# Last layer of a graph network: dot products over halves of a turn, additions interleaved, chain operations joined, eight tail buffers

## The reference, cut to what matters

```
def _agg(entity_emb, relation_emb, head, tail, relation_type):
    head_emb, tail_emb, rel_emb = entity_emb[head], entity_emb[tail], relation_emb[relation_type]
    ricci = _l2_normalize(tail_emb + rel_emb)
    hyper_head = expmap0(head_emb)
    hyper_tail = expmap(tail_emb, hyper_head)
    hyper_rel = expmap(rel_emb, hyper_head)
    res = project(mobius_add(hyper_tail, hyper_rel))
    res = logmap(res, hyper_head) + ricci * 1e-07
    res = jax.nn.relu(res)
    sums = jnp.zeros((n_entities, res.shape[-1]), res.dtype).at[head].add(res)
    ...
```

## Time and profile before

| what | value |
|---|---|
| timed, median of 3 runs | 5223.61 us (5222.07 to 5224.58) |
| profiled execution, span | 6351.7 us |
| DVE busy | 3726.5 us, 59% |
| POOL busy | 3463.1 us, 55% |
| PE busy | 2842.1 us, 45% |
| ACT busy | 1728.7 us, 27% |

### The profile page before, as it was taken

How to read it: one execution, slowest core, us unless ns; L and a number is a source line. 1 busy time by engine, 2 the same in 40 slices (tenths; PEclk the granted TensorE clock), 3 DMA queues, 4 the chain that set the end, 5 groups by cost and what they waited for, 6 DMA issues and landing times. The chain is left out here.

```text
span 6351.7 us, 75027 instructions
## 1 busy us (share of the span) xinstructions
PE 2842.1 (45%) x17919; PEld 2271.2 (36%) x17920; DVE 3726.5 (59%) x6870; ACT 1728.7 (27%) x5084; POOL 3463.1 (55%) x3375
## 2 busy tenths in 40 slices
PE   4544588433343334477614434434431343444442
PEld 1333456223333333345403333333331233333332
DVE  6444544255555666444426776667673767667678
ACT  0255200011111111000003354344340335445434
POOL 5667445466555663544265565566525556556551
PEclk7655699666666666678855555555555555555555
DMA  3720400355555554400021111111102111111110
GB/s 101 171 94 1 127 1 1 105 154 172 167 171 169 173 173 143 139 4 1 8 49 42 37 42 37 37 41 38 33 10 50 40 37 42 37 39 41 41 30 13
DMA packets 470914, 446.71 MB, mean 70 GB/s; under 512 B 113322, under 2 KB 417773, under 8 KB 470268
## 3 DMA queue, kind: packets, MB, share of 16 engines
q1 hardware_dynamic: 230602, 227.94, 12.4%
q0 software_dynamic: 116768, 136.51, 9.0%
q10 hardware_dynamic: 123282, 79.08, 4.5%
HBM read 306.93 MB, written 136.34 MB: 70 GB/s over the span
## 5 line engine op out<-in xcount | busy, mean ns | idle before, releaser
L2412 POOL DMA_INDIRECT tg<-tab_d,tail_ids x1632 | 1711.2, 1049 | 1191.1 <-DVEq L2731 644.9
L458 POOL DMA_INDIRECT sorted_edges_d<-place_batch x784 | 825.0, 1052 | 657.1 <-issue 220.6
L2437 PE MATMUL hr<-near_table,near_hot 128*128 x4896 | 654.4, 278 | 926.2 <-issue 593.1
L1598 POOL DMA_INDIRECT xg<-tab_d,src_i x784 | 768.0, 980 | 501.1 <-issue 241.6
L2445 PE MATMUL acc<-msg,sum_hot 128*96 128x65 f32 x3264 | 559.8, 364 | 902.1 <-ACT msg L2519 701.3
L2437 PEld LDWEIGHTS hr<-near_table,near_hot 128*128 128x128 f16 x4896 | 505.6, 108 | 1075.7 <-issue 970.2
L2445 PEld LDWEIGHTS acc<-msg,sum_hot 128*96 128x96 f32 x3264 | 536.4, 277 | 924.8 <-issue 924.7
L2492 ACT ACTIVATE pr<-hr 128x396 f32<-128x396 f32 x576 | 272.2, 482 | 1235.0 <-DMA b2col<-in_L_gnn_be_dram 786.9
L2513 ACT ACTIVATE pr<-pr,coef_c 128x64 f32<-128x64 f32 x1496 | 380.7, 340 | 82.4 <-issue 79.4
L2506 ACT ACTIVATE msg<-tg,coef_b 128x64 f32<-128x64 f32 x1632 | 399.1, 340 | 2.6 <-DVEq L2926 2.6
L2743 DVE TENSOR_REDUCE scal<-prod 128x17 f32<-128x1088 f32 x288 | 370.5, 1286 | 9.8
(11 more groups left out here) (504 smaller groups left out, 5392.9 us busy)
## 6 DMA issues: line engine op xcount, KB each, us to landing
ex<-spread_d SPq DMA_DIRECT2D x112, 448.0 KB
msg_d<-back ACTq DMA_DIRECT2D x112, 448.0 KB
near_hot<-head_row_d SPq DMA_DIRECT2D x96, 408.0 KB
tg<-tab_d,tail_ids POOLq DMA_INDIRECT x1632
spread_d<-zeros ACTq DMA_DIRECT2D x28, 896.0 KB
spread_d<-zeros SPq DMA_DIRECT2D x28, 896.0 KB
idsU<-dst_short_d SPq DMA_DIRECT2D x112, 224.0 KB
pairs_d<-pair_m SPq DMA_DIRECT2D x3, 4800.0 KB
```

The source lines that it names most:

```text
L458: l.eng.indirect_dma_start(K.sorted_edges[:, :], bass.IndirectOffsetOnAxis(ap=K.batch[:, n % 2, 0, k:k + 1], axis=0), K.batch[:, n % 2, 1, ...
L1598: l.eng.indirect_dma_start(xg[j.c % ROWS][:, half * H + k, :], None, K.tab1, bass.IndirectOffsetOnAxis(ap=src_i[:, t:t + 1], axis=0)).then ...
L2412: e.indirect_dma_start(tg[:, u % TAILS * GQ + k, :], None, K.tab3, bass.IndirectOffsetOnAxis(ap=K.tail_ids[:, u * GQ + k:u * GQ + k + 1], ...
L2437: ins = e.matmul(hr[(u * FILLS + g) % 2][:, c:c + PW3], near_hot[u % HOTS][:, k, :], rows[:, bass.ds(at[k] + n * PW3, PW3)], start=n == 0, ...
```

## The change

1. `TAILS` is 8 in place of 9. Four quarters are then always contiguous in `tg`, and a turn's tails are one slice `T_`.
2. `dot` goes over halves: one product of 128x2176 and one reduction for two quarters. `prod` is one tile of the size of the former two. The marks stay as many: one after each half.
3. `gather_up` handles a whole turn. The quarter's operations are split (`sum_keys`, `add_heads`, `add_kinds`), and between the two additions of a quarter stands another operation: the `sum_hot` of the next quarter, a `near_hot`, or its own `sum_hot`.
4. In the chain, operations of the same kind on neighbouring rows of `scal` are joined, some rows are moved so that they are neighbours, and the copies into `scal` are three in place of ten; one of them copies the heads' squared lengths (`PP`), which were read with a stride of 132 elements before. B and C are written to one tile, `coef_bc`.

```
-TAILS = 9
+TAILS = 8
...
+        def gather_up(p, n, mark):
+            sum_keys(p)
+            add_heads(p)
+            sum_keys(p + 1)
+            add_kinds(p)
+            mark()
+            add_heads(p + 1)
+            if n is not None:
+                near(n)
+            add_kinds(p + 1)
+            mark()
+            if n is not None:
+                near(n + 1)
+            for u in (p + 2, p + 3):
+                add_heads(u)
+                sum_keys(u)
+                add_kinds(u)
+                mark()
...
-            def dot(n, x, y, quarters, taken=False, landed=False):
-                for q in quarters:
-                    u = now + q
+            def dot(n, x, y, halves, taken=False, landed=False):
+                for h in halves:
+                    at = slice(2 * h * GQ, (2 * h + 2) * GQ)
+                    u = now + 2 * h + 1
                     if taken:
                         v.wait_ge(near_taken, (u + 1) * FILLS)
                     if landed:
-                        v.wait_ge(got[u % TAILS], 16 * GQ * (u // TAILS + 1))
+                        for w in (u - 1, u):
+                            v.wait_ge(got[w % TAILS], 16 * GQ * (w // TAILS + 1))
                     v.wait_ge(l.sem, l.done())
-                    tt_(prod[q % 2][:, :, :], x(q), y(q), MUL)
+                    tt_(prod[:, :, :], x[:, at, 0:D], y[:, at, 0:D], MUL)
                     v.wait_ge(l.sem, l.done())
-                    v.tensor_reduce(sc[:, n, q * GQ:(q + 1) * GQ], prod[q % 2][:, :, :], AX.X, ADD).then_inc(l.sem, l.add(1))
-                    if q % 2 == 1:
-                        mark()
+                    v.tensor_reduce(sc[:, n, at], prod[:, :, :], AX.X, ADD).then_inc(l.sem, l.add(1))
+                    mark()
...
-            tt0(a2, a2, u2, MUL)
-            tt_(b2, b2, u2, MUL)
+            ab2 = sc[:, 10:14, :].rearrange("p (n two) m -> p n two m", two=2)
+            tt_(ab2, ab2, u2.unsqueeze(1).to_broadcast([P, 2, 2, M]), MUL)
...
-            for c in (cA, cB, cC):
-                tt_(c, c, f, MUL)
+            tt0(abc, abc, three(f), MUL)
```

More of the change, by code:

```diff
@@ L2343, in edge_loop3 @@
     tg = sb("tg3", [P, TAILS * GQ, RW], F32)
-    prod = two("prod3", [P, GQ, D], F32)
+    prod = sb("prod3", [P, 2 * GQ, D], F32)
     msg = [sb(f"msg3{q}", [P, GQ, D + 1], F32) for q in range(QN)]
@@ L2347, in edge_loop3 @@
     cA, cB, cC = (sc[:, n, :] for n in (26, 27, 28))
-    kB, kC = (two(n, [P, M], F32) for n in ("coef_b", "coef_c"))
-    terms = prod[0][:, :, :].rearrange("p k f -> p (k f)")[:, 0:9 * M].rearrange("p (n m) -> p n m", m=M)
+    coef_bc = two("coef_bc", [P, 2, M], F32)
+    kB, kC = ([c[:, n, :] for c in coef_bc] for n in range(2))
+    terms = prod[:, :, :].rearrange("p k f -> p (k f)")[:, 0:9 * M].rearrange("p (n m) -> p n m", m=M)
     zero = pr[1][:, 0:2, :].rearrange("p k f -> p (k f)")[:, 0:256].bitcast(F16)
@@ L2569, in near, with sum_keys @@
             v.tensor_scalar(hot, hot, K.lane_id[:, 0:1], None, ALU.is_equal).then_inc(near_made, 1)
-        def gather_up(u):
-            s, t = turn(u)
+        def sum_keys(u):
             if u >= 2:
@@ L2576, in gather_up, with add_heads @@
                             names.unsqueeze(1).to_broadcast([P, GQ, BN]), ALU.is_equal).then_inc(sum_made, 1)
-            p_, r_, out = pr[s][:, t, 0:D], pr[s][:, t, RW:RW + D], msg[u % QN][:, :, 0:D]
+        def add_heads(u):
+            s, t = turn(u)
+            p_, out = pr[s][:, t, 0:D], msg[u % QN][:, :, 0:D]
             tt_(p_, p_, kA[s][:, t].unsqueeze(2).to_broadcast([P, GQ, D]), MUL)
@@ L2581, in gather_up, with add_kinds @@
             tt_(out, out, p_, ADD)
+        def add_kinds(u):
+            s, t = turn(u)
+            r_, out = pr[s][:, t, RW:RW + D], msg[u % QN][:, :, 0:D]
             if u < QUARTERS - QN:
@@ L2698, in vector, with form @@
         both = lambda x: x.unsqueeze(1).to_broadcast([P, 2, M])
-        def form(out, A, B, C, PP_, pt, pr, tr, q2):
+        def form(out, abc, heads, tr, q2):
+            A, B, C = (abc[:, n, :] for n in range(3))
             x = [terms[:, n, :] for n in range(9)]
-            tt0(x[0], B, pt, MUL)
-            tt0(x[1], C, pr, MUL)
-            tt0(x[2], A, PP_, MUL)
+            tt0(terms[:, 0:3, :], abc, heads, MUL)
             tt0(x[3], C, tr, MUL)
-            tt0(x[4], B, q2[:, 0, :], MUL)
-            tt_(x[5], C, C, MUL)
+            tt_(terms[:, 4:6, :], abc[:, 1:3, :], q2, MUL)
             l.eng.wait_ge(l.sem, l.done())
-            tt0(x[6], x[0], x[1], ADD)
+            tt0(x[6], x[1], x[2], ADD)
             st0(x[7], x[3], 2.0, x[4], MUL, ADD)
-            tt_(x[8], x[5], q2[:, 1, :], MUL)
+            tt_(x[8], x[5], C, MUL)
             l.eng.wait_ge(l.sem, l.done())
-            st0(x[0], x[6], 2.0, x[2], MUL, ADD)
+            st0(x[0], x[6], 2.0, x[0], MUL, ADD)
             tt_(x[1], B, x[7], MUL)
@@ L2738, in dot @@
                     if landed:
-                        v.wait_ge(got[u % TAILS], 16 * GQ * (u // TAILS + 1))
+                        for w in (u - 1, u):
+                            v.wait_ge(got[w % TAILS], 16 * GQ * (w // TAILS + 1))
                     v.wait_ge(l.sem, l.done())
-                    tt_(prod[q % 2][:, :, :], x(q), y(q), MUL)
+                    tt_(prod[:, :, :], x[:, at, 0:D], y[:, at, 0:D], MUL)
                     v.wait_ge(l.sem, l.done())
-                    v.tensor_reduce(sc[:, n, q * GQ:(q + 1) * GQ], prod[q % 2][:, :, :], AX.X, ADD).then_inc(l.sem, l.add(1))
-                    if q % 2 == 1:
-                        mark()
+                    v.tensor_reduce(sc[:, n, at], prod[:, :, :], AX.X, ADD).then_inc(l.sem, l.add(1))
+                    mark()
                 v.wait_ge(l.sem, l.done())
-            head = lambda q: P_[:, q * GQ:(q + 1) * GQ, 0:D]
-            kind = lambda q: R_[:, q * GQ:(q + 1) * GQ, 0:D]
-            tail = lambda q: tg[:, tails(now + q), 0:D]
+            T_ = tg[:, s * M:(s + 1) * M, :]
             def ask_scalar(k):
@@ L2756, in ask_scalar @@
                 v.wait_ge(answered, j * NA + k)
[L2757 to L2768, removed]
+            dot(dPR, P_, R_, range(2), taken=True)
+            dot(dPT, P_, T_, range(1), landed=True)
+            dot(dTR, T_, R_, range(1))
+            if not first:
+                gather_up(p, None if last else n, mark)
+            else:
+                near(n)
+                near(n + 1)
+                v.sem_inc(paced, QN)
+            dot(dPT, P_, T_, range(1, 2), landed=True)
+            dot(dTR, T_, R_, range(1, 2))
             PT, PR, TR, d2 = A1(dPT), A1(dPR), A1(dTR), A2(dPT)
-            q2, n2, s2, t2, u2, a2, b2, X2 = A2(24), A2(2), A2(4), A2(6), A2(8), A2(10), A2(12), A2(14)
+            PP, heads, abc = A1(dPT - 1), sc[:, dPT - 1:dPT + 2, :], sc[:, 26:29, :]
+            q2, n2, s2, t2, u2, a2, b2, X2 = A2(2), A2(24), A2(4), A2(6), A2(8), A2(10), A2(12), A2(14)
             ask = A2(0)
             om = A1(23)
[L2773 to L2778, removed]
+            both_of = lambda x: x.rearrange("p k c -> p c k")
+            v.tensor_copy(sc[:, 2:25:22, :], both_of(T_[:, :, D:D + 2]))
+            v.tensor_copy(sc[:, 3:26:22, :], both_of(R_[:, :, D:D + 2]))
+            v.tensor_copy(PP, PP_)
             ts_(om, PP_, -1.0, 1.0, MUL, ADD)
@@ L2793, in vector @@
             tt0(a2, t2, u2, ADD)
-            tt_(X2, u2, both(PP_), MUL)
+            tt_(X2, u2, both(PP), MUL)
             l.eng.wait_ge(l.sem, l.done())
@@ L2803, in vector @@
             mark()
-            tt0(a2, a2, u2, MUL)
-            tt_(b2, b2, u2, MUL)
+            ab2 = sc[:, 10:14, :].rearrange("p (n two) m -> p n two m", two=2)
+            tt_(ab2, ab2, u2.unsqueeze(1).to_broadcast([P, 2, 2, M]), MUL)
             l.eng.wait_ge(l.sem, l.done())
             tt0(t2, b2, d2, MUL)
-            tt_(u2, a2, both(PP_), MUL)
+            tt_(u2, a2, both(PP), MUL)
             l.eng.wait_ge(l.sem, l.done())
@@ L2841, in vector @@
             mark()
-            tt0(A1(6), A1(6), A1(18), MUL)
-            tt_(A1(7), A1(7), A1(18), MUL)
+            tt_(A2(6), A2(6), both(A1(18)), MUL)
             l.eng.wait_ge(l.sem, l.done())
[L2845 to L2848, removed]
+            tt_(sc[:, 25:29, :].rearrange("p (n two) m -> p n two m", two=2), A2(6).unsqueeze(1).to_broadcast([P, 2, 2, M]), ab2, MUL)
             l.eng.wait_ge(l.sem, l.done())
-            tt_(cA, A1(16), A1(17), ADD)
+            tt_(cA, A1(25), cA, ADD)
             l.eng.wait_ge(l.sem, l.done())
             yy = A1(29)
-            form(yy, cA, cB, cC, PP_, PT, PR, TR, q2)
+            form(yy, abc, heads, TR, q2)
             mark()
@@ L2862, in vector @@
             ask_scalar(2)
-            v.reciprocal(A2(18), ask).then_inc(l.sem, l.add(1))
+            v.reciprocal(X2, ask).then_inc(l.sem, l.add(1))
             l.eng.wait_ge(l.sem, l.done())
-            f, g = A1(18), A1(19)
+            f, g = A1(14), A1(15)
```

(15 more changed lines are left out.)

17 lines of the change are left out of this document (6 added, 11 removed).

## The result

| what | before | after |
|---|---|---|
| timed, median of 4 runs | 5224.09 us (5222.07 to 5228.17) | 5347.09 us (5344.01 to 5354.90) |
| ratio, 95% interval | | 1.0235 [1.0222, 1.0248] |
| profiled execution, span | 6351.7 us | 5353.3 us |

The change makes the kernel 2.35% slower; 5342 us were predicted. One correction belongs here, since every later comparison hangs on it. The same kernel before takes some 5230 us in some sessions on a chip and 6314 to 6354 us in others, timed as well as profiled there. Its profile, with its span of 6351.7 us, is of the second kind; the times above and the profile after are of the first. I call them the quick and the stalling kind. Ratios are always taken within a session; turns are compared only within a kind. The number of the chip doesn't tell the kinds apart: one session of either kind had the same one.

The account below looks back on a forecast made before the run. POOL's gathers were taken to set the turn, 92.1 us against DVE's 91.3; 23 turns by 5.5 us more (126), less 8 at the hops' ends, added to 5223.6 gave about 5342 us, range 5120 to 5430.

Parts of the forecast that it names:

- Taking the stalls out of the turn: DVE's profiled turn of 116.4 us, less 25.9 of stalls plus 0.8 for two answers, gives 91.3 us.
- POOL binds before: In the kernel before, POOL's 68 gathers take 92.1 us and set the turn, DVE less than 1 us behind.
- What holds a gather: A DVE operation with two SBUF operands holds a 0.95 us gather until it ends; reductions, casts and PSUM reads do not.
- second case: POOL binds but its gather delay doesn't change; only the hops' ends gain, 5216 us; chance 0.11.
- Dots over halves: Twelve product-reduction pairs become six of 4.99 us: DVE saves 2.7 us a turn, POOL gains 4.8 to 12.3 us of delay.
- The tenth of the way to two gathers: Some third gathers miss a half's open stretch, raising POOL's turn from 96.9 to 97.6 us, 5.5 above 92.1.
- The additions' order and the joined operations: In gather_up and chain, DVE saves 0.8 and 2.3 us a turn; the additions' order costs POOL nothing (-1.5 to +1).
- The sum: DVE's turn falls 5.8 to 85.5 us, POOL's rises 5.5: 126 us over 23 turns, less 8 at hops' ends, about 5342.
- Rival (A), the saving shows: Gathers never bind and DVE's saving shows, 24 turns by 3.5 us: 84 less, 5140 us; chance 0.34.

Follow-up runs that it names:

- Quarters back: The changed kernel with its dots over quarters again, the rest of the change kept: 5243.15 us, ratio 1.0026 to the kernel before.
- halves alone: The kernel before with dots over halves and eight tail buffers, old chain and old order of additions: 5351.06 us, ratio 1.023.
- Chain alone: The kernel before with the joined chain and eight buffers, dots over quarters, additions in old order: ratios 0.9975, 0.9897 and 0.9992 in three stalling sessions.

## Why the prediction was right, and where it was not

- **Taking the stalls out of the turn: right, for a wrong reason.** I read them as belonging to the profiled execution. They belong to the session, timed runs too. Removing them was right because the timed runs were of the quick kind; beside runs of the other kind it would have misled. The turn that was left holds: DVE's 85.5 us are 96.3 - 11.1 = 85.2 after. So the forecast started from the right turn by luck.
- **POOL binds before: shown nearly.** Quarters back has 92.0 us against the 92.1 worked out, POOL without a pause, and 1.1 to 6.8 us a turn of waiting for landed rows; DVE's turn without them is 87.5. The kernel before itself was never profiled in the quick kind.
- **What holds a gather: right for the products, with gaps beside them.** 2.19 and 2.34 us under products, 0.94 beside reductions, 0.95 under a product that reads PSUM; in the profile before, the prediction's sum of 0.95 and what is left 0.13 us after the start fits all 383 gathers that ran into a product or an addition, within 0.04 us. But two SBUF operands aren't the whole condition. `near_hot` reads one tile and one number per partition, and its 0.79 us hold a gather too, which took 1.47 (first two rows, the kernel before); and beside the 96-row casts of 2.42 us, which let gathers through at 0.95, there are 32-row casts of 1.32 us ahead of the first hop's turns, under which gathers took 2.73 and 2.01. In a turn `near_hot` costs POOL 0.2 to 0.6 us, so the sum doesn't hang on it.

```profile
3764.43 0.79 DVE L2569 TENSOR_SCALAR near_hot<-near_hot,lane_id 128x2176 f16<-128x2176 f16 x1 [0.15 <-issue]
3764.56 1.47 POOL L2412 DMA_INDIRECT tg<-tab_d,tail_ids  x1 [0.30 <-issue]
```

```profile
2943.56 0.98 DVE L2569 TENSOR_SCALAR near_hot<-near_hot,lane_id 128x2176 f16<-128x2176 f16 x1
```

The Trainium skill's inference that tensor_tensor leaves descriptor generation alone (SBUF — State Buffer, "Who interferes with whom") is contradicted again. The prediction called what that inference would give its second case; but with POOL at 85.1 us and DVE at 91.3 it would have been the first, DVE setting the turn. Both are refuted, 5140 and 5216 us. The rule that whoever starts first keeps the pair stands in the same section of the Trainium skill for instructions of DVE in a 2-port mode. Products don't show it: begun inside a gather they keep 2.42 us. `near_hot` does, a little: it took 0.98 us in place of 0.79 where it began 0.54 us into a gather (last row, halves alone).
- **Dots over halves: mechanism right, size a little high.** The pair takes 4.99 us and lets three gathers in, as predicted. Added up over the gathers, products delay POOL by 7.6 us a turn after and by 2.9 with quarters back, where 7.4 and 2.6 were worked out: 4.7 against 4.8. The tenth of the way to two gathers, which made 5.5 of it, has no counterpart: the turn grew by 4.4, and hardly a third gather misses. DVE's own turn got 87.5 - 85.1 = 2.4 us shorter by halves, where 2.7 were expected.
- **The additions' order and the joined operations: DVE's 3.1 us are there, POOL's nothing is wrong.** Between halves alone and after, DVE's turn falls from 88.4 to 85.1 us, by 3.3; 1.2 of these are `sum_hot`'s wait for PE, which the prediction didn't have in its sum. But a mean gather grows from 1.110 to 1.115 us and the mean turn from 96.0 to 96.4, 8 us over 22 turns, which takes back what the hops' ends gain (ratios of 1.023 and 1.0235). Quarters back should have gained some 8 us at the hops' ends and lost 12. Its turns vary between 89.3 and 94.6 us, so a gather's mean moves with where the gathers fall. Chain alone has the shorter gathers, by 0.011 us against the kernel before, so the joined operations and the buffers don't look like what costs, and the additions' order does; but that was seen in stalling sessions, where POOL waits, and it was not separated in the quick kind.
- **The sum.** The spans of after and quarters back differ by 111 us: 22 x 4.4 = 98 in the turns, 4 between the hops and 5 in the first turn make 107 for halves. The last 4.5 lie ahead of the last layer, where both run the same code (its first gather starts at 2815.50 and 2811.02), and are chance. With 12 for the rest that is some 119 to 123. 5.5 x 23 - 8 = 118 hit it by two errors of opposite sign: 126 us for halves in place of 107, and a gain of 8 us that turned out as a loss of 12. That it came so close is luck; the step of 4.8 us is not.
- **Rival (A), the saving shows: excluded by POOL.** The prediction put the limit at a pitch of about 1.1 us, but 68 gathers exceed 85.5 us from 85.5 / 68 = 1.26 on; the kernel after has 1.115 + 0.30 = 1.42. With gathers taken out, DVE's turn is 87.3 us: 85.2 and some 2 us of waiting for ScalarE at the chain's first answer, where I had put 3. The grouping that the Trainium skill advises for a saturated engine (Perfetto Trace Analysis, "Optimizing Scalar/DVE Operations") did shorten DVE's path, by 2.4 and 3.3 us in the quick profiles, and the time went to POOL.

What is open: what makes a session stall. In the stalling kind the layers ahead of the last take longer too: the last one's first gather starts at some 3205 us in the profile before, against 2815.30 in halves alone, whose code is the same up to there.

## What to carry to other kernels

Before DVE operations are joined, ask who waits for their end: here a gather that began under a long product with two SBUF operands did, and when gathers have no slack, the length of the blocked stretch and how many gathers fit into the open one set the time. Saving DVE's own work was worth nothing here and stays so until the gathers become fewer or shorter. If a profile is longer than the timed runs, run the kernel again with times and a profile in one session before removing anything from it.

## What the runs showed of the hardware beyond this

One kernel took 5231 us in one session and 6314 to 6354 in three others. In one of the latter PE starts matmuls of 0.27 us 1.42 us apart after a long run of gathers, and is at its pace 2.2 us after they pause; a fifth fewer gathers took 6.6% off the time.
